# A four-layer graph network on one core: two products moved to ScalarE, a row load moved back, weight rows spread through DRAM, two steps of layer 3 moved

## The chip, the cores and the metric

The kernel runs on one core of a Trainium2 chip. The metric is the device time of one execution in microseconds. Three runs of the kernel before gave 1193.82, 1193.92 and 1194.11 us; the median, 1193.92 us, is the time that the prediction starts from. TensorE (PE) multiplies matrices, VectorE (DVE) and ScalarE (ACT) work on tiles element by element, SyncE (SP) issues nearly all transfers, and 16 DMA engines carry them.

## What is computed

Four graph layers with a residual each, over N = 4096 nodes with D = 128 features and a 4096 x 4096 float32 adjacency of which about one entry in a thousand is not zero.

```python
h = relu(layernorm(x)); x = x + L0(h, adj)   # weighted mean over neighbours, then W and relu
h = relu(layernorm(x)); x = x + L1(h, adj)   # 2 attention heads, layernorm, ff, elu
h = relu(layernorm(x)); x = x + L2(h, adj)   # 1 attention head
h = relu(layernorm(x)); x = x + L3(h, adj)   # adj.T @ h, divided by the column sums
# attention: e = leaky_relu(src[:, None] + dst[None, :]); e = where(adj > 0, e, -9e15)
#            out = softmax(e, axis=1) @ h
```

## The kernel before, in words

**Tiling.** The adjacency is cut into T = 32 tiles of 128 rows along the contracted side and Q = 4 quarters of 1024 columns. A pass of the kernel runs over one quarter and, inside it, over k = 0 to 31. There are five such layers of passes, numbered by `h`: 0 is the reference's L0, 1 and 2 are the two heads of its L1, 3 is its L2, 4 its L3. In this text "layer 0" to "layer 4" are these. In layers 0 and 3 the adjacency tile is the stationary operand, and a tile takes 8 products with 129 columns of G (`products`, L539). In layers 1, 2 and 4 G is stationary, and a tile takes two products with 512 columns (`wide_products`, L555). A float32 product is two instructions, so a tile is 16 instructions of the narrow kind or 4 of the wide.

**Layer 0.** SP loads the tile of k (512 KB) into one of eight slots of the mask area; for the last quarter, where that area fills up, the slots are given by hand (`HOMES`): parts of `ring`, of `U` and of idle parts of `G`. PE multiplies with it, and DVE turns it into an 8-bit mask that is kept on the chip (`masks`, L1405) and from which layers 1 to 3 build their attention tiles. SP loads the tile of k only when PE has used and DVE has masked the tile of k - 8: both engines hold the loads back.

**Attention.** DVE makes a tile E of exponentials with one instruction, max(row, rank) times mask (`run` of DVE, L1367), into one of 4 or 5 slots; PE consumes it and gives the slot back. `row` is a row of scores broadcast over the partitions, and G is scaled in each partition by an exponential v (`scale_g`). At the first quarter of layers 1 and 3 the scores of the last quarter of nodes are not known yet. So tiles 0 to 23 (`EARLY` = 24) go by an early maximum, and before tile 24 the late steps make the right maximum (`top_of`), scale the last part of G (`scale_g(h, 3)`), and correct the running sums (`scale_sums`, L1305 and L1316). The raw row for this is loaded twice, for the early part and as `late_home` for the late one (`load_raw`, L422).

**Hooks.** Each engine's program is one list. `at(ks, steps)` hangs the steps of other work (the last quarter's normalisation, statistics, projections) behind tile k of the running pass, in the order given; the lists `ks` are written by hand. Post-work of a quarter runs over DVE, ACT and PE by turns: for instance the statistics of `post1` (DVE), a root (ACT), `scal` (DVE, L1185), a normalisation (ACT, L829), a transpose on PE (`turned`, L570).

**The weights' rows.** At the second quarter of layer 0, PE's hook 3 projects the weights, and DVE's hook 4 (`place_back`) puts four columns of 128 values into `qcol`. PE's hook 6 (`spread_dots`, L703 and L566) transposes each column, broadcast, into PSUM, so that every partition has it as a row, and DVE's hook 9 (`keep_dots`, L1429) copies the rows to the chip's memory. DVE's dot products of layer 1's feed (`dots`, L1216, from hook 17 on) read them.

Of the kernel before, what the change touches and what calls it, by code (L numbers as in the profile page):

```python
# [30 lines left out]
P = 128  # L31
ALU = mybir.AluOpType
ACT = mybir.ActivationFunctionType
F32 = mybir.dt.float32
# [30 lines left out]
def graph_layers(nc, x, adj, adj_t, diag, alpha, w0_t, bias0, ff0, ff0_t, ff1_t, attn, g1, b1, g2, b2,  # L65
                 w2, w2_t, a2, out, inputs1):
    N, D = x.shape
    T = N // P
    Q = 4
    S = T // Q  # L70
# [19 lines left out]
    with ExitStack() as ctx:  # L90
# [3 lines left out]
        def sem(name):  # L94
            return ctx.enter_context(nc.semaphore(name))
# [8 lines left out]
        ident = sb("ident", [P, P])  # L104
        given_blocks = nc.dram_tensor("given_blocks", (P, T * P), U8, kind="Internal").ap()
        given_rows = nc.dram_tensor("given_rows", (3, N), F32, kind="Internal").ap()
        raw_rows = nc.dram_tensor("raw_rows", (2, QC), F32, kind="Internal").ap()
        ff1T = sb("ff1T", [P, HEADS, D])
        score1 = sb("score1", [P, T, 4])
# [98 lines left out]
        f_var, f_dev, f_scale, f_norm = sem("f_var"), sem("f_dev"), sem("f_scale"), sem("f_norm")  # L208
        f2_var, f2_dev, f2_scale, f2_in = sem("f2_var"), sem("f2_dev"), sem("f2_scale"), sem("f2_in")
        h_turned, h_wide, h_projected, h_placed = sem("h_turned"), sem("h_wide"), sem("h_projected"), sem("h_placed")  # L210
        dots_spread, dots_kept = sem("dots_spread"), sem("dots_kept")
        f_turned, f_wide, f_projected, f_placed = sem("f_turned"), sem("f_wide"), sem("f_projected"), sem("f_placed")

        top_placed, top_spread, bias_made, row_shifted = sem("top_placed"), sem("top_spread"), sem("bias_made"), sem("row_shifted")
# [133 lines left out]
        def _(sp):  # L348
# [15 lines left out]
            def layer0(q, some=range(T)):  # L364

                L = FIRST
                for k in some:
                    if q > 0 and k == 12:
                        keep_own(q - 1)
                    if last_of(q):  # L370
                        home, before = HOMES[k], last_in(HOMES[k], k)
                        if before is not None:
                            sp.wait_ge(*read0(q, before))
                            sp.wait_ge(mask_made, q * T + before + 1)
                        elif home >= MASK:
                            sp.wait_ge(*read0(q - 1, T - FIRST + home - MASK))
                            sp.wait_ge(mask_made, q * T - FIRST + home - MASK + 1)
                        elif home == SUMS:
                            sp.wait_ge(post_done, q)
                    elif k >= L:  # L380
                        sp.wait_ge(slot_used, q * (T - 1) + k - L + 1)
                        sp.wait_ge(mask_made, q * T + k - L + 1)
                    elif 0 < q:
                        if k == L - 1:
                            sp.wait_ge(acc_summed[NB - 1], q)
                        else:
                            sp.wait_ge(slot_used, q * (T - 1) + k - L + 2)
                        sp.wait_ge(mask_made, q * T + k - L + 1)
                    sp.dma_start(tile0(q, k), span(adj_t[k * P:(k + 1) * P, :], q * QC, QC)).then_inc(loaded0(q, k)[0], 16)
# [31 lines left out]
                sp.wait_ge(raw_written, 16 * fixes[h])  # L421
                sp.dma_start(home, raw_rows[fixes[h] - 1].partition_broadcast(P)).then_inc(raw_loaded, 16)  # L422

            layer0(1)
            layer0(2, range(FIRST))
            write_raw(1)
            layer0(2, range(FIRST, T))
            layer0(3, range(2 * S + 2))
            sp.wait_ge(slot_used, (Q - 1) * (T - 1) + S)
            load_raw(1, rows_home[1, 0])  # L430
            layer0(3, range(2 * S + 2, 3 * S + 2))
            sp.wait_ge(slot_used, (Q - 1) * (T - 1) + 2 * S)
            load_raw(1, late_home[1])
            layer0(3, range(3 * S + 2, T))


            sp.wait_ge(f_placed, 2 * Q - 1)
# [92 lines left out]
        def _(pe):  # L530
# [33 lines left out]
            def spread(col, dst):  # L564

                return pe.transpose(dst, col.broadcast_to([P, P]), ident[:, :])  # L566
# [63 lines left out]
            def run(h, q, hooks):  # L630
                n = q + h * Q
                for k in range(T):
                    if h == 0:
                        pe.wait_ge(*loaded0(q, k))
                        if fixed(q) and q == 0 and k < S:
                            if k < HALF - 1:
                                pe.wait_ge(h_placed, k + 1)
                            elif k <= HALF:
                                pe.wait_ge(f_norm if k < HALF else f_placed, 1)
                        elif fixed(q) and q == 0 and k % S == 0:  # L640
                            pe.wait_ge(f_placed, k // S + 1)
                        lhs, used = tile0(q, k), slot_used
                    elif h == 4:
                        pe.wait_ge(*deep(q, k))
                        if fixed(q) and q == 0 and k % S == 0:
                            pe.wait_ge(f_norm, 4 * Q + k // S + 1)
                        lhs, used = stream3[:, k % DEEP, :], deep_used
                    else:
                        pe.wait_ge(e_made, (n - Q) * T + k + 1)
                        if fixed(q) and q == 0 and k % S == 0:  # L650
                            if h == 2:
                                pe.wait_ge(f_norm, 2 * Q + k // S + 1)
                            else:
                                pe.wait_ge(g_scaled[k // S], fixes[h])
                        lhs, used = edges(h, q)[k % len(edges(h, q))], e_used
                        if k == 0 and h != 2 and not (fixed(q) and q == 0):
                            pe.wait_ge(fixed_v, fixes[h])
                    fix = fixes[h] if h in fixes and fixed(q) and q == 0 else 0
                    before = None if fixed(n) and n == 0 else taken(h, q - 1) if not (fixed(q) and q == 0) else taken(h - 1, Q - 1)
                    if h in (1, 2, 4):  # L660
                        wide_products(before, k, lhs, G[:, h % 2, k, 0:P], used, fix)
                    else:
                        products(before, k, lhs, G[:, h % 2, k, :], used, fix, narrow_after=fixed(n) and n == 3 * Q)
                    if k in hooks:
                        hooks[k]()
# [38 lines left out]
                pe.matmul(mix[:, 2, 0:4], affine, qv[:, 0:4], start=True, stop=True, skip_group_check=True)\  # L704
                    .then_inc(back_summed, 1)

            def spread_dots():
                pe.wait_ge(back_placed, 1)
                for c in range(4):
                    mm = spread(qcol[:, c:c + 1], mix[:, 0, c * P:(c + 1) * P])  # L710
                mm.then_inc(dots_spread, 1)
            run(0, 1, {3: turn_weights_back, 6: spread_dots})
            for q in range(2, Q - 1):
                run(0, q, {})
            run(0, Q - 1, {23: lambda: spread_top(early_top[1])})
# [102 lines left out]
        def _(act):  # L818
# [127 lines left out]
            def early_exponentials(h):  # L946

                s_ = SLOPE[h]
                act.wait_ge(bias_made, early_top[h])
                act.activation(G[:, h % 2, 0:EARLY, D], rank[h][:, 0:EARLY], ACT.Exp, bias=vbias, scale=s_).then_inc(v_made, 1)  # L950
                act.activation(rank[h][:, 0:EARLY], rank[h][:, 0:EARLY], ACT.Exp, bias=wbias, scale=1.0 - s_).then_inc(w_made, 1)
                row_exponentials(h, rows_home[h, 0], kept_rows[h] - 1)
# [140 lines left out]
            act.wait_ge(affine_made, 1)  # L1093
            quarters(act, 1, Q - 1, stage0)
            early_exponentials(1)


            post0(Q - 1)
# [53 lines left out]
        def _(dve):  # L1152
# [165 lines left out]
            def scale_g(h, part):  # L1318

                if part == 0:  # L1320
                    dve.wait_ge(v_made, early_top[h])
                elif part == Q - 1:
                    dve.wait_ge(v_made, late_top[h])
                gp = G[:, h % 2, part * S:(part + 1) * S, :]
                v = gp[:, :, D:D + 1].broadcast_to([P, S, D])
                dve.tensor_tensor(gp[:, :, 0:D], gp[:, :, 0:D], v, ALU.mult).then_inc(g_scaled[part], 1)
# [92 lines left out]
            def place_back():  # L1419
# [4 lines left out]
                for c, i in enumerate((1, 3, 0, 2)):  # L1424
                    ins = dve.tensor_copy(qcol[:, c:c + 1], mix[:, 2, i:i + 1])
                ins.then_inc(back_placed, 1)
            def keep_dots():
                dve.wait_ge(dots_spread, 1)
                dve.tensor_copy(w0T, mix[:, 0, 0:P])  # L1429
                dve.tensor_copy(spare[:, o:o + 3 * D], mix[:, 0, P:4 * P]).then_inc(dots_kept, 1)  # L1430
                dve.wait_ge(dots_kept, 1)

            def small_turn(p):

# [40 lines left out]
            def stage0(q, more={}):  # L1475
                post, fed = post0(q - 1), feed(1, q - 1 + Q, q - 1)
                ks = [2,3,5,6,20,7,8,9,10,10,12,14,15,17,18] if last_of(q) else [2, 3, 5, 6, 22, 7, 8, 10, 12, 12, 14, 17, 19, 20, 22]
                masks(q, beside(at(ks, post + fed), more))
            stage0(1, {4: place_back, 9: keep_dots})
            quarters(dve, 2, Q - 2, stage0, st, STAGE0)  # L1480
            early = early_of(1)
            stage0(Q - 1, {21: early[0], 24: early[1], 30: lambda: scale_g(1, 0), 31: lambda: scale_g(1, 1)})


            def post1(h, q):
# [112 lines left out]
                dve.wait_ge(mean_spread, 1)  # L1598
                dve.tensor_copy(mean2, mixed[:, 0:D]).then_inc(mean_kept, 1)
            last = post1(1, Q - 1)  # L1600
            ks = [3,4,5,7,8,14,14,14,16,17,21,22,23,24,25,27]
            run(3, 0, at(ks, last + feed(3, 4 * Q - 1, Q - 1) + late_steps(3) + [mean_of_all, keep_mean]))


# [124 lines left out]
```

## Time and profile before

| what | value |
|---|---|
| median of three runs | 1193.92 us |
| the profiled execution's own time | 1193.39 us |
| its span, first to last instruction | 1191.6 us |
| PE matmuls busy | 1185.7 us, 100% |
| DVE busy | 938.3 us, 79% |
| ACT busy | 325.5 us, 27% |
| granted TensorE clock, mean | 1.000 |
| DMA engines busy, by 40 slices | 8 or 9 tenths in the first eight slices (layer 0) and in the last quarter, 0 to 3 between |

Span and own time differ by 1.8 us, which lie around the first and the last instruction. A busy share says which engine to look at, not what one edit is worth. That is read from the timeline around the edit: which engine waits there, for what, and what comes next.

### The profile page before, as it was taken

Reading aid. Unit: us, or ns where it says so; the run is one execution under the profiler, and the core shown is the slowest. Engines: PE = TensorE matmul, PEld = TensorE weight load, DVE = VectorE, ACT = ScalarE, POOL = GpSimd, SP = SyncE. Lnnn points to the kernel's source line nnn. Section 1 sums busy time; section 2 is a strip of 40 time slices with the busy share of each in tenths; the row PEclk is TensorE's granted clock in tenths of the full one; section 3 lists DMA queues with packets and bytes.
Section 4 is the critical chain, followed back from the end, with each engine's and each line's share of the span. In section 5 each row is a group of like instructions: output and inputs, shape, how many; then the busy total and the mean of one; then the engine's idle time right before and its main releaser. Section 6 shows DMA issues by size and latency. Waiting matters only on the chain.

```text
span 1191.6 us, 16721 instructions
## 1 busy us (share of the span) xinstructions
PE 1185.7 (100%) x6235; PEld 816.7 (69%) x6235; DVE 938.3 (79%) x1677; ACT 325.5 (27%) x780; POOL 9.6 (1%) x20
## 2 busy tenths in 40 slices
PE   9999999999999999999999999999999999999999
PEld 9999999954444444444454547999999964444455
DVE  5548585798979787889797787788787869887786
ACT  4512122225323242423445234541212121000000
POOL 3000000000000000000000000000000000000000
DMA  9888898800111102110010101032303068999920
GB/s 324 304 279 291 248 347 305 282 29 15 40 18 37 18 35 35 53 18 22 1 22 0 40 1 40 1 108 90 141 0 141 1 268 304 313 329 322 322 82 18
DMA packets 90227, 156.30 MB, mean 131 GB/s; under 512 B 45904, under 2 KB 54448, under 8 KB 90160
## 3 DMA queue, kind: packets, MB, share of 16 engines
q1 hardware_dynamic: 64240, 148.58, 36.3%
q10 hardware_dynamic: 25456, 6.30, 2.4%
q8 instruction: 42, 0.69, 0.2%
q0 software_dynamic: 464, 0.53, 0.2%
q14 instruction: 25, 0.20, 0.1%
HBM read 146.94 MB, written 4.78 MB: 127 GB/s over the span
## 4 chain that ended last, share of the span: by engine, by line
PE 94%; DVE 4%; ACT 1%; DMA 0%; issue 0%; DVEq 0%; ACTq 0%
PE acc L555 48%; PE acc L539 36%; PE acc L802 4%; DVE ring L1367 2%; PE mix L621 1%; PE mix L593 1%; PE mix L608 1%; PE acc L810 1%; PE turn L570 1%; DMA ring<-in_adj_t 0%; DVE G L1367 0%; PE mix L670 0%; ACT V L829 0%; DVE stats L1170 0%; ACT U L829 0%
## 5 line engine op out<-in xcount | busy, mean ns | idle before, releaser
L1367 DVE SCALAR_TENSOR_TENSOR ring<-G,score,mask 128x1024 f32<-128x1024 f32 x372 | 466.8, 1280 | 70.9 <-PE acc L555 38.7
L555 PE MATMUL acc<-ring,G 128*128 128x512 f32 x1000 | 436.3, 593 | 0.3 <-DVE acc L1305 0.2
L555 PEld LDWEIGHTS acc<-ring,G 128*128 128x128 f32 x1000 | 186.5, 190 | 229.6 <-issue 210.9
L539 PE MATMUL acc<-G,ring 128*128 128x129 f32 x2240 | 253.9, 275 | 0.8 <-DVE acc L1316 0.7
L539 PEld LDWEIGHTS acc<-G,ring 128*128 128x128 f32 x2240 | 251.9, 192 | 2.1 <-DVE ring L1367 2.0
L539 PE MATMUL acc<-G,mask 128*128 128x129 f32 x1648 | 185.8, 275 | 0.0
L539 PEld LDWEIGHTS acc<-G,mask 128*128 128x128 f32 x1648 | 184.8, 192 | 0.0
L555 PE MATMUL acc<-mask,G 128*128 128x512 f32 x384 | 165.8, 593 | 0.0
L1637 DVE TENSOR_TENSOR ring<-ring,mask 128x1024 f32<-128x1024 f32 x120 | 146.8, 1223 | 11.0 <-DVE ring L1637 0.5
L555 PEld LDWEIGHTS acc<-mask,G 128*128 128x128 f32 x384 | 72.6, 190 | 91.0 <-issue 89.8
L1405 DVE TENSOR_SCALAR mask<-mask 128x1024 uint8<-128x1024 f32 x103 | 68.4, 689 | 27.4 <-DMA mask<-in_adj_t 26.8
L841 ACT ACTIVATE dev<-var 128x8 f32<-128x8 f32 x28 | 5.9, 210 | 217.0 <-DVE var L1179 217.0
L1023 ACT COPY U<-acc 128x512 f32<-128x512 f32 x22 | 12.9, 586 | 172.1 <-PE acc L555 172.1
L802 PE MATMUL acc<-mask,G 128*128 128x384 f32 (+1 forms) x128 | 48.6, 540 | 0.0
L1031 ACT COPY U<-acc 128x387 f32<-128x387 f32 (+1 forms) x24 | 10.4, 446 | 131.6 <-PE acc L539 130.8
L802 PEld LDWEIGHTS acc<-mask,G 128*128 128x128 f32 x128 | 24.2, 190 | 24.0 <-issue 15.6
L829 ACT ACTIVATE V<-X,shift,scale 128x128 f32<-128x128 f32 (+1 forms) x88 | 35.1, 480 | 0.0
L825 ACT ACT_TABLE_LOAD x26 | 33.4, 1283 | 2.7 <-ACT V L829 1.6
L821 ACT COPY cols<-ident 128x1 f32<-128x1 f32 x40 | 7.6, 190 | 86.0 <-DVE V L1216 23.4
L829 ACT ACTIVATE V<-U,shift,scale 128x128 f32<-128x128 f32 x64 | 25.5, 481 | 5.2 <-DVE shift L1189 5.2
L1216 DVE SCALAR_TENSOR_TENSOR V<-G,ring 128x128 f32<-128x128 f32 x96 | 21.4, 290 | 5.3 <-ACT G L829 5.2
L1405 DVE TENSOR_SCALAR mask<-ring 128x1024 uint8<-128x1024 f32 x18 | 12.1, 690 | 10.7 <-PE acc L539 8.7
(207 smaller groups left out, 707.0 us busy)
## 6 DMA issues: line engine op xcount, KB each, us to landing
mask<-in_adj SPq DMA_DIRECT2D x128, 512.0 KB, 5.5
mask<-in_adj_t SPq DMA_DIRECT2D x103, 512.0 KB, 5.2
ring<-in_adj_t SPq DMA_DIRECT2D x18, 512.0 KB, 6.4
G<-given_rows SPq DMA_DIRECT2D x10, 512.0 KB, 3.9
G<-in_adj_t SPq DMA_DIRECT2D x4, 512.0 KB, 6.4
G<-raw_rows SPq DMA_DIRECT2D x4, 512.0 KB, 5.2
inputs<-V ACTq DMA_DIRECT2D x4, 512.0 KB, 2.7
V<-inputs SPq DMA_DIRECT2D x4, 512.0 KB, 3.9
```

The lines of the kernel that those rows point to most:

```text
L539: mm = pe.matmul(acc[:, b, (s % 3) * DW:(s % 3) * DW + DW], lhs[:, s * P:(s + 1) * P], g, start=(k == 0 and s % 3 == 0), stop=(k == T - 1) ...
L555: mm = pe.matmul(acc[:, c, :], g, moving[:, c * BANK:(c + 1) * BANK], start=(k == 0), stop=(k == T - 1), skip_group_check=True)
L570: mm = pe.transpose(turn[:, s * P:(s + 1) * P], V[:, s, :], ident[:, :])
L593: mm = pe.matmul(dst, U[:, s * P:(s + 1) * P], weights, start=True, stop=True, skip_group_check=True)
L802: mm = pe.matmul(acc[:, c, 0:n], G[:, 0, k, 0:P], stream3[:, k, c * BANK:c * BANK + n], start=(k == 0), stop=(k == T - 1), skip_group_chec ...
L825: act.activation(warm[func], ident[:, 0:1], func)
L829: ins = act.activation(dst(s), src(s), func, bias=add(s), scale=mul(s))
L1023: act.copy(U2[:, c, :], acc2[:, c, :]).then_inc(acc_taken, 1)
L1216: ins = dve.scalar_tensor_tensor(V[:, s, :], blocks(G[:, 1, :, :], q, 1, s)[:, 0, 0:D], 1.0, dot_w[c], ALU.mult, ALU.mult, accum_out=block ...
L1367: dve.scalar_tensor_tensor(slots[k % L], late_home[h] if early and k >= EARLY else rows_home[h, q], rank[h][:, k:k + 1], span(mask, (q * T ...
L1405: dve.tensor_scalar(span(mask, (q * T + k) * QC, QC), tile0(q, k), 0.0, None, ALU.is_gt).then_inc(mask_made, 1)
L1637: dve.tensor_tensor(added, stream3[:, 0, :] if k == 1 else added, stream3[:, k, :], ALU.add).then_inc(tile_added, 1)
```

## The change

Four edits, quoted below with the lines that matter.

1. **G of layer 1.** The products of its parts 0 and 1 with v are taken from the end of DVE's list in the last quarter of layer 0 (hooks 30 and 31, one instruction each over 1024 columns) and given to ACT behind the early exponentials, in 8 instructions of 128 columns each for a part.
2. **The late raw row.** SP issued its load between tiles 25 and 26 of the last quarter of layer 0; it now issues it behind tile 31.
3. **The weights' rows.** PE's four transposes and DVE's two copies go. SP writes `qcol` to DRAM as four rows, behind tile 15 of the second quarter, issues tiles 16 and 17, waits until the write has landed, and loads the rows back, broadcast to all partitions, in two transfers. DVE waits for them at the hook at which it had copied, 9.
4. **Layer 3, first quarter.** On DVE the step `scal` moves from hook 8 to 7, and the late step with the maximum (`top_of`) and `scale_g(3, 3)` come at hook 23 together (before: 22 and 23).

```diff
+        dot_rows = nc.dram_tensor("dot_rows", (4 * P,), F32, kind="Internal").ap()
@@ SP
-            layer0(1)
+            layer0(1, range(T // 2))
+            sp.wait_ge(back_placed, 1)
+            sp.dma_start(dot_rows.rearrange("(c p) -> p c", p=P), qcol, allow_slow_non_contiguous=True).then_inc(dots_written, 16)
+            layer0(1, range(T // 2, T // 2 + 2))
+            sp.wait_ge(dots_written, 16)
+            sp.dma_start(w0T, dot_rows[0:P].partition_broadcast(P)).then_inc(dots_loaded, 16)
+            sp.dma_start(spare[:, o:o + 3 * D], dot_rows[P:4 * P].partition_broadcast(P)).then_inc(dots_loaded, 16)
+            layer0(1, range(T // 2 + 2, T))
@@ SP
-            layer0(3, range(2 * S + 2, 3 * S + 2))
+            layer0(3, range(2 * S + 2, T))
             sp.wait_ge(slot_used, (Q - 1) * (T - 1) + 2 * S)
             load_raw(1, late_home[1])
-            layer0(3, range(3 * S + 2, T))
@@ PE
-            def spread_dots():
-                pe.wait_ge(back_placed, 1)
-                for c in range(4):
-                    mm = spread(qcol[:, c:c + 1], mix[:, 0, c * P:(c + 1) * P])
-                mm.then_inc(dots_spread, 1)
-            run(0, 1, {3: turn_weights_back, 6: spread_dots})
+            run(0, 1, {3: turn_weights_back})
@@ ACT
             early_exponentials(1)
+            scale_g(1, 0)
+            scale_g(1, 1)
@@ DVE
-            def keep_dots():
-                dve.wait_ge(dots_spread, 1)
-                dve.tensor_copy(w0T, mix[:, 0, 0:P])
-                dve.tensor_copy(spare[:, o:o + 3 * D], mix[:, 0, P:4 * P]).then_inc(dots_kept, 1)
-                dve.wait_ge(dots_kept, 1)
+            def dots_there():
+                dve.wait_ge(dots_loaded, 32)
@@ DVE
-            stage0(1, {4: place_back, 9: keep_dots})
+            stage0(1, {4: place_back, 9: dots_there})
-            stage0(Q - 1, {21: early[0], 24: early[1], 30: lambda: scale_g(1, 0), 31: lambda: scale_g(1, 1)})
+            stage0(Q - 1, {21: early[0], 24: early[1]})
@@ DVE, run(3, 0)
-            ks = [3,4,5,7,8,14,14,14,16,17,21,22,23,24,25,27]
+            ks = [3, 4, 5, 7, 7, 14, 14, 14, 16, 17, 21, 23, 23, 24, 25, 27]
```

## Rows read from the trace of the kernel before

**Rows 1.** The page, part 1: busy time, share of span, instructions.
```profile
PE 1185.7 (100%) x6235; PEld 816.7 (69%) x6235; DVE 938.3 (79%) x1677; ACT 325.5 (27%) x780; POOL 9.6 (1%) x20
```

**Rows 2.** Timeline of PE: start us, us, engine, line, tiles, [idle before <-releaser].
```profile
246.87 3.60 PE L555 MATMUL acc<-ring,G 128*128 128x512 f32 x8
250.31 1.88 PE L555 MATMUL acc<-G 128*128 128x512 f32 x4
...
268.46 1.98 PE L555 MATMUL acc<-G 128*128 128x512 f32 x4 [0.82 <-DVE G L1367]
...
279.54 1.09 PE L582 MATMUL turn<-ident,G 128*128 128x128 f32 x8
...
746.72 1.09 PE L570 MATMUL turn<-ident,V 128*128 128x128 f32 x8 [0.43 <-ACT V L829]
...
777.59 2.05 PE L539 MATMUL acc<-G,ring 128*128 128x129 f32 x16
...
780.49 3.95 PE L539 MATMUL acc<-G,ring 128*128 128x129 f32 x32 [0.74 <-DVE acc L1316]
```

**Rows 3.** Timeline of PE around the four transposes of the weights' rows.
```profile
87.31 0.60 PE L566 MATMUL mix<-ident,ring 128*128 128x128 f32 x4
87.75 52.42 PE L539 MATMUL acc<-G,mask 128*128 128x129 f32 x468
```

**Rows 4.** Timeline of DVE, second quarter of layer 0: hook 9, masks 10 and 13.
```profile
90.84 0.28 DVE L1429 COPY ring<-mix 128x128 f32<-128x128 f32 x1
...
91.63 0.69 DVE L1405 TENSOR_SCALAR mask<-mask 128x1024 uint8<-128x1024 f32 x1
...
98.77 1.29 DVE L1405 TENSOR_SCALAR mask<-mask 128x1024 uint8<-128x1024 f32 x2
```

**Rows 5.** Views of lines L417 and L389: raw row's write, then the tile of 136.2.
```profile
L417 SPq DMA_DIRECT2D raw_rows<-score x1: 426/426/426, 133.0 to 133.0; - x1
DMA to landing us min/median/max: 9.8/9.8/9.8
...
DMA to landing us min/median/max: 10.7/10.7/10.7
```

**Rows 6.** The same view: the 28 tiles issued from 80 to 130 us.
```profile
DMA to landing us min/median/max: 4.4/4.8/5.8
```

**Rows 7.** The same view: the tile issued at 224.0, into an empty queue.
```profile
DMA to landing us min/median/max: 3.8/3.8/3.8
```

**Rows 8.** Timeline of DVE, end of layer 0, start of layer 1.
```profile
240.51 0.69 DVE L1405 TENSOR_SCALAR mask<-ring 128x1024 uint8<-128x1024 f32 x1 [0.59 <-DMA ring<-in_adj_t]
...
242.85 1.22 DVE L1326 TENSOR_TENSOR G<-G 128x1024 f32<-128x1024 f32 x1
243.99 2.48 DVE L1367 SCALAR_TENSOR_TENSOR ring<-G,score,mask 128x1024 f32<-128x1024 f32 x2
...
247.58 2.48 DVE L1367 SCALAR_TENSOR_TENSOR ring<-G,score,mask 128x1024 f32<-128x1024 f32 x2
```

**Rows 9.** Timeline of ACT in the same stretch.
```profile
246.03 1.41 ACT L1031 COPY U<-acc 128x387 f32<-128x387 f32 x3 [9.83 <-PE acc L539]
...
256.45 2.43 ACT L983 ACTIVATE G<-G 128x128 f32<-128x128 f32 x8
```

**Rows 10.** Timeline of DVE, first quarter of layer 3, around hooks 7 and 8.
```profile
741.85 1.28 DVE L1367 SCALAR_TENSOR_TENSOR ring<-G,score,mask 128x1024 f32<-128x1024 f32 x1
743.04 0.20 DVE L1185 RECIPROCAL scale<-dev 128x8 f32<-128x8 f32 x1
```

**Rows 11.** Timeline of DVE and ACT, the same quarter, around hooks 22 to 24.
```profile
773.40 0.16 DVE L1269 TENSOR_REDUCE cols<-score 128x1 f32<-128x8 f32 x1 [2.17 <-ACT score L939]
...
776.26 1.28 DVE L1367 SCALAR_TENSOR_TENSOR ring<-G,score,mask 128x1024 f32<-128x1024 f32 x1
...
779.78 1.36 DVE L1316 TENSOR_TENSOR acc<-acc,ring 128x387 f32<-128x387 f32 x3
...
776.38 1.06 ACT L944 ACTIVATE G<-G 128x1024 f32<-128x1024 f32 x1
```

More of the change, by code:

```diff
@@ L210, in graph_layers @@
         h_turned, h_wide, h_projected, h_placed = sem("h_turned"), sem("h_wide"), sem("h_projected"), sem("h_placed")
-        dots_spread, dots_kept = sem("dots_spread"), sem("dots_kept")
+        dots_written, dots_loaded = sem("dots_written"), sem("dots_loaded")
         f_turned, f_wide, f_projected, f_placed = sem("f_turned"), sem("f_wide"), sem("f_projected"), sem("f_placed")
```

## The prediction

> **What bounds the kernel.** I read the page first, then the timeline of PE for gaps, and last the timelines of DVE, ACT and SP around each gap. PE is busy for 1185.7 us [rows 1] of the 1191.6 us span, and its clock is at full level. So an edit pays only if it takes instructions off PE or closes one of its gaps. The gaps are few. In layer 1, the 8 wide matmuls of two tiles take 250.31 - 246.87 = 3.44 us [rows 2], 1.72 a tile. Tile 12 is due at 246.87 + 12 x 1.72 = 267.5 and starts at 268.46 [rows 2], 0.96 late. The turn behind tile 17 is due at 246.87 + 18 x 1.72 = 277.8 and starts at 279.54 [rows 2], 1.7 late. In layer 3, PE waits 0.43 for ACT before the turn at 746.72, then for tile 23 (777.59, some 0.25 late), then 0.74 for the corrected sums (780.49) [rows 2]. With the time until the next first matmul, the layer 3 gaps come to 0.59, 0.25 and 0.90. Elsewhere PE is fed: 468 narrow matmuls in 52.42 us are 0.112 us each [rows 3], which 16 to a tile makes 1.79 us.
>
> **Part A, PE's four transposes.** They start at 87.31 and the next matmul at 87.75 [rows 3]: 0.44 us of PE, with nothing beside it. Gain 0.44, certain.
>
> **Part B, what takes their place.** This is SP, DRAM and a wait on DVE, and the cost has to be worked out as a chain; times are on the clock of before, PE 0.44 early. PE's tile 7 starts at 87.3 and ends at 89.1; SP issues tile 15 then and the element write at about 89.8. The trace has one such write in the same setting, the raw row's: 1024 values of 4 bytes at 133.0, landed 9.8 us later; the tile issued 3.2 us behind it took 10.7 [rows 5] against 4.8 in the calm stretch [rows 6], so 5.9 more. Ours has 512 values. If the hold-up goes by the count, it is half: landed 5.9 us after issue or so (2 us to get through the queue, half of the other 7.8), at 95.7; tile 17, issued at 92.9, lands at 92.9 + 4.8 + 2.9 = 100.6. The two loads are issued at 96, stand behind it in the queue, and 256 KB are half a tile. **The rows are there at about 101**, between 98 (write soon through) and 107 (below).
>
> Before, mask 10 came at 91.63 [rows 4]. So DVE stands at hook 9 for some 9 us. Behind it are the masks, and behind those SP's loads, since tile k needs mask k - 8. From mask 10 to mask 13 are 98.77 - 91.63 = 7.14 us, with ACT's normalisation between, and 0.6 for mask 13 itself [rows 4]: tile 21 can be issued 8.0 us after the rows are there. By then the queue is empty, and a tile takes 3.8 [rows 7], so it lands 11.9 us after them with the signal. PE wants tile 21 at 87.31 + 14 x 1.79 = 112.3. **The point from which this wait counts is therefore rows at 100.4**; at 101 it costs 0.6 us. Tiles 18 to 20 have 2 us or more of slack; from tile 22 on the loads follow at 1.3 us or less against PE's 1.79, so the stall is paid once. DVE's two copies (from 90.84 to 91.63 [rows 4]) are saved where DVE waits anyway: nothing. Cost of B: 0.6, from 0 to 6.4.
>
> **Part C, start of layer 1.** The first tile E starts at 243.99, when both products (the second at 242.85, 1.14 us) are done [rows 8]. Without them E0 comes behind mask 31. That needs tile 31's landing. Tile 30 landed at 240.5 [rows 8]; mask 31 ran right behind the first product at 242.25, so tile 31 was there by then, and without the raw row ahead of it not later. With mask 31 at 242.25 still, E0 would start at 242.85, 1.14 early. With landing at 241.0, E0 to E3 are made by 246.5, and E4 waits for its slot until PE has read its tile 31 (some 0.2 behind 246.87 [rows 2], so 247.1), where before it ended at 247.58 + 2.4 = 249.97 [rows 8]: 248.3, 1.67 early. DVE is busy without a gap from there to PE's stalls, so **the chain comes 1.1 to 1.7 early, I take 1.5**, since moving the 512 KB row away frees about 1.3 us of the queue ahead of the last tiles. PE can use up to 1.7 (above). What is late next is the turn behind tile 17, by 0.2. Gain C: 1.5.
>
> The cover of the moved work: ACT makes 8 instructions for a part in 2.43 us [rows 9], so both take 4.9 us. It stood idle for 9.83 us before 246.03 [rows 9], behind one copy of 1.15 us; both fit, and PE needs part 0 at 246.87 only. Without that cover, all 4.9 us would stand ahead of the copy of the sums that PE waits for at the start of layer 1. On the rows ACT needs 2.43 us for what DVE does in 1.14. The Trainium skill ("ScalarE: Activation LUTs", Rules for kernel authors) says that multiplications belong on VectorE, which is faster per element. By that rule the edit would lose 2.6 us if ACT were bound here; the trace agrees with the rule on the price, and the idle time makes it free.
>
> The late raw row is now issued near 237 and first used by the late step, which comes behind the turn of 279.54 [rows 2]; it is late for nobody. SP's commands behind it (the weight of layer 3, the last own blocks) shift by less than a microsecond.
>
> **Part D, layer 3.** `scal` at hook 7: DVE now waits about 0.5 us for ACT's root instead of making E8 first (741.85), and the scale comes at about 742.35 in place of 743.04 [rows 10]. ACT's normalisation and PE's turn follow 0.7 earlier, and the gap of 0.59 closes. E8 ends near 743.9; PE wants it at 746.72 - 0.59 - 1.79 = 744.3. The late step at hook 23: DVE stood idle for 2.17 us before 773.40 [rows 11], and E23 now fits there, so PE does not wait for it (0.25). Behind the maximum, at 776.26 [rows 11], come the product (1.14) and E24, which needs ACT's row at 777.44 [rows 11]: 777.5 to 778.7. The sums are corrected from 778.7, not from 779.78 [rows 11], and PE, which ends tile 23 at 777.34 + 1.79 and turns the rows in 0.11, starts tile 24 at 779.25 rather than 780.49. Then E25 is made only at 781.2 and PE is there at 781.0: 0.2 comes back, against 0.2 that PE lost there before. Gain D: 0.59 + 1.24 = 1.8; bounds 1.0 (E8 or E25 late by 0.8 together) and 2.0.
>
> **Sum** against the profiled execution's own 1193.39: -0.44 + 0.6 - 1.5 - 1.8 = -3.1, which gives 1190.3. The median lies 0.53 above the profiled one, so **1190.8 us**. A difference that can be told from none is 0.2%, 2.4 us.
>
> **Rivals.**
>
> 1. *The element write does not go by its count.* If the 4-byte writes queue for the same stretches of memory, 512 hold up the engines as long as 1024 did. Then the write lands at 99.6 and tile 17 at 92.9 + 10.7 = 103.6 [rows 5], the rows are there at about 104.4, and PE stalls for 4.0 at tile 21. Sum: -0.44 + 4.0 - 3.3 = +0.3, so 1194.2, no difference. For it: the trace has no write of another count; against it: nothing but the plausibility of a cost per value. The Trainium skill ("DMA: Bandwidth & Descriptors", Queues, rings and completion order) says that a transfer's signal lands only after all earlier writes of the same DMA engine. The trace agrees as far as it goes: the tile behind the raw write landed late too [rows 5].
> 2. *Slower: DVE's wait at hook 9.* If in addition the loads, issued only when the write has landed (99.6), take the 7 us that a transfer has in a disturbed queue (the mean of 3.8 [rows 7] and 10.7 [rows 5]), the rows are there at 106.8. DVE's wait holds mask 13, mask 13 holds tile 21, and PE stalls for 106.8 - 100.4 = 6.4. Sum: -0.44 + 6.4 - 3.3 = +2.7, 1196.6. It ends slower than before from rows at 104.1, slower by 0.2% from 106.5. Against it: small reads behind a write that has landed stand in a calm queue.
> 3. *The wait is hidden.* If the write lands in 4 us, the rows come by 100 and B costs nothing; with C at 1.67: -0.44 - 1.7 - 1.9 = -4.0, 1189.9.
> 4. *C or D does not do what it says*: another link of the chain (ACT's root, the slot of an E tile) holds PE at the same place. With half of 3.3 lost, 1192.4, no difference.
>
> **How the numbers follow.** Forecast (B between 0 and 1.3) 0.42, rival 3 0.15, rival 1 (stall of 1.3 to 5) 0.22, rival 4 0.12, rival 2 0.09. The forecast's own spread is 1190.2 to 1191.5, just under the threshold of 1191.5. Faster by over 0.2%: 0.42 and 0.15, 0.57. Within: rivals 1 and 4, 0.34. Slower: rival 2, 0.09. The range goes from 1189.8 (rival 3) to 1194.4 (rival 1), and leaves out rival 2 and the upper tail of rival 1.
>
> **What would show it.** In the changed trace: no transposes at 87 and PE's tiles 0.44 early; DVE idle before mask 10 with a DMA as releaser, for about 9 us; a PE gap at tile 21 of the second quarter, waiting for a DMA, of about 0.6; the first E tile 1.1 to 1.7 earlier against PE's first wide matmul, and no PE gap at tile 12; no gap at the turn of layer 3, and tile 24 some 1.2 us earlier against tile 22. The prediction is wrong if the rows arrive after 102, if ACT's products delay its copy of layer 0's last sums, or if E8 or E25 now hold PE.

## The result and the profile after

| kernel | median, us | against before |
|---|---|---|
| before, in the runs beside it | 1194.01 | 1 |
| the whole change | 1197.24 | 1.0031 (95% interval 1.0023 to 1.0039) |

**Slower by 3.2 us, where 3.1 us faster was forecast.** The profiled execution of the changed kernel took 1198.24 us with a span of 1196.4. The kernel before was measured again beside each group of runs, and its median moved by up to 1.1 us between them (1192.88 to 1194.01); so each kernel is compared with the runs of the kernel before made beside it.

PE's timeline of the second and third quarter of layer 0, after the change (start us, us, engine, line, tiles, [idle before <-releaser]):

```profile
83.27 25.26 PE L546 MATMUL acc<-G,mask 128*128 128x129 f32 x224
111.07 2.05 PE L546 MATMUL acc<-G,mask 128*128 128x129 f32 x16 [2.54 <-DMA mask<-in_adj_t]
113.59 3.84 PE L546 MATMUL acc<-G,mask 128*128 128x129 f32 x32 [0.47 <-DMA mask<-in_adj_t]
118.58 7.56 PE L546 MATMUL acc<-G,mask 128*128 128x129 f32 x64 [1.16 <-DMA mask<-in_adj_t]
126.32 13.89 PE L546 MATMUL acc<-G,mask 128*128 128x129 f32 x122 [0.17 <-DMA mask<-in_adj_t]
...
152.41 17.77 PE L546 MATMUL acc<-G,mask 128*128 128x129 f32 x154 [0.81 <-DMA mask<-in_adj_t]
```

From tile 4 at 83.27 the four transposes are gone [rows 3], and 14 tiles run through. Then PE waits for tiles 18, 19, 21 and 25. Tile 25 is due at 83.27 + 21 x 1.787 = 120.8 and starts at 126.32: **5.5 us lost in the second quarter**. Tile 7 of the third is due 14 tiles later, at 151.3, and starts at 152.41: 1.1 more, and 0.3 follow at the tiles behind it. Before, nothing was lost in either [rows 3]. A check on the whole is PE's next instruction that is no product with a tile. It comes 84 tiles after tile 4, in the last quarter; here in the changed kernel, and before together with tile 4:

```profile
240.36 0.27 PE L573 MATMUL mix<-ident,cols 128*128 128x128 f32 x1
```
```profile
81.87 5.61 PE L539 MATMUL acc<-G,mask 128*128 128x129 f32 x48
...
232.47 0.27 PE L566 MATMUL mix<-ident,cols 128*128 128x128 f32 x1
```

It comes 240.36 - 83.27 = 157.09 us behind tile 4, before 232.47 - 81.87 = 150.60 with the 0.44 of the transposes in it. **So 6.9 us are lost in layer 0, some 5.5 in the second quarter and 1.4 in the third.**

DVE's timeline at hook 9, and the view of the transfers of the rows:

```profile
91.64 0.69 DVE L1409 TENSOR_SCALAR mask<-mask 128x1024 uint8<-128x1024 f32 x1
106.48 0.69 DVE L1409 TENSOR_SCALAR mask<-mask 128x1024 uint8<-128x1024 f32 x1 [14.15 <-DMA ring<-dot_rows]
```
```profile
L427 SPq DMA_DIRECT2D dot_rows<-ring x1: 427/427/427, 91.1 to 91.1; - x1
L430 SPq DMA_DIRECT2D ring<-dot_rows x1: 327/327/327, 101.0 to 101.0; - x1
L431 SPq DMA_DIRECT2D ring<-dot_rows x1: 426/426/426, 101.3 to 101.3; - x1
...
DMA to landing us min/median/max: 4.0/5.1/9.9
```

The write (L427) took the 9.9 us; the loads were issued when it had landed and took 4.0 and 5.1 us, and DVE stood for 14.15 us where before it copied for 0.8 and went on [rows 4].

The start of layer 1 and the first quarter of layer 3, PE and one row of DVE:

```profile
250.54 2.48 DVE L1371 SCALAR_TENSOR_TENSOR ring<-G,score,mask 128x1024 f32<-128x1024 f32 x2 [0.21 <-DVE mask L1409]
```
```profile
254.77 3.60 PE L562 MATMUL acc<-ring,G 128*128 128x512 f32 x8
...
286.13 1.09 PE L589 MATMUL turn<-ident,G 128*128 128x128 f32 x8
...
750.93 1.95 PE L546 MATMUL acc<-G,ring 128*128 128x129 f32 x16
752.72 1.04 PE L577 MATMUL turn<-ident,V 128*128 128x128 f32 x8
...
785.33 3.95 PE L546 MATMUL acc<-G,ring 128*128 128x129 f32 x32
```

The first E tile stands 254.77 - 250.54 = 4.23 us ahead of PE's first wide matmul, before 246.87 - 243.99 = 2.88 [rows 2, 8]. From that matmul to the turn behind tile 17 are 31.36 us, before 279.54 - 246.87 = 32.67 [rows 2]: **1.3 gained**. In layer 3 the turn follows its tile by 1.79, which is no gap (0.59 before), and from the turn to tile 24 are 32.61 us, before 33.77 [rows 2]: **1.75 gained**. So the sum of the profiled executions is -0.44 + 6.9 - 1.3 - 1.75 = +3.4. The rest of their difference of 4.85 lies ahead of the change: tile 4 of the second quarter starts at 83.27, before at 81.87, 1.4 earlier. That start lay between 81.3 and 83.8 in the profiles of this study, whichever edits a kernel had.

### The profile page after: what moved, and what is told of

The parts are those of the page before. It is cut to its first block, busy times and chain, and to the rows that moved or that the text cites. A ratio compares the mean times of both kernels' runs of the same rounds, so it can differ in the third digit from the quotient of the medians.

```text
span 1196.4 us, 16728 instructions
## 1 busy us (share of the span) xinstructions
PE 1186.1 (99%) x6231; PEld 816.1 (68%) x6231; DVE 935.0 (78%) x1673; ACT 331.0 (28%) x796; POOL 9.6 (1%) x20
## 4 chain that ended last, share of the span: by engine, by line
PE 90%; DMA 5%; DVE 3%; ACT 1%; issue 0%; DVEq 0%; ACTq 0%
PE acc L562 48%; PE acc L546 33%; DMA mask<-in_adj_t 4%; PE acc L804 4%; PE mix L628 1%; DVE ring L1371 1%; PE mix L615 1%; PE mix L600 1%; PE acc L812 1%; ACT U L866 0%; DMA ring<-in_adj_t 0%; PE turn L577 0%; DVE G L1371 0%; ACT G L831 0%; PE mix L677 0%; ACT V L831 0%
## 5 line engine op out<-in xcount | busy, mean ns | idle before, releaser
L1058 ACT ACTIVATE U<-V,cols 128x512 f32<-128x512 f32 x8 | 6.1, 808 | 51.6 <-DMA V<-U 51.6
```

## The experiments

Each kernel below has one profiled execution, and sizes of gaps are from that one; the times are medians where nothing else is said. Code is cut to the lines that matter.

Theory: the way through DRAM is the loss, by DVE's wait, the masks and SP's loads; the three other edits do what they say. Rivals: another edit costs as well, or the slow write holds the tiles up whatever DVE does.

### Edits 1, 2 and 4 without the way through DRAM

Against the changed kernel (PE's function and SP's lines of edit 3 are put back as well):

```diff
-            run(0, 1, {3: turn_weights_back})
+            run(0, 1, {3: turn_weights_back, 6: spread_dots})
...
-            stage0(1, {4: place_back, 9: dots_there})
+            stage0(1, {4: place_back, 9: keep_dots})
```

> Edits 1, 2 and 4 alone: the weights' rows are spread by PE and copied by DVE as before. Theory (the slowdown is the way through DRAM: DVE's wait for the rows at hook 9 holds the masks and by them SP's tile loads, and PE stalls 5 to 6 us in layer 0; the other edits do what they say): 1191.0 us, 3.0 below before, with no PE gap over 0.5 us in the second quarter of layer 0, none at tile 12 of layer 1 and none before the turn of layer 3. Rival (one of the other edits costs time as well): 1193 us or more.

Measured 1190.65 us against 1193.24, ratio 0.9978 (0.9969 to 0.9987). PE's waits, all of them:

```profile
PE mix L669 <- DVE V L1376: 1.1, 1, 1.1
PE mix L592 <- ACT U L863: 0.7, 1, 0.7
PE acc L538 <- DMA mask<-in_adj_t: 0.3, 1, 0.3
PE acc L554 <- DVE acc L1306: 0.2, 1, 0.2
```

The waits of layers 1 and 3 of before [rows 2] are gone; the one for a tile's DMA is in the first quarter, at 27.6 us, and the second has none. The other edits are a gain of 2.6 us; the rival about them falls.

### Edit 3 alone

> Edit 3 alone. Theory: PE stalls at tiles 18 to 31 of the second quarter, 5 to 6 us in sum, less 0.44 for the transposes: 1199.0 us, 5 above before, and the gaps of layers 1 and 3 as before. Rival (the stalls are shared between this edit and the others): under 1197 us.

Measured 1199.44 us against 1193.24, ratio 1.0049 (1.0035 to 1.0062): 6.2 us, where 5 were expected. Its profile shows less than the expected 5 to 6 us in the second quarter, 3.8, and 1.4 that were not expected in the third; that is 4.8 with the transposes taken off, so over a microsecond of the 6.2 is not found in these gaps (the interval runs from 4.2 to 7.4). The two runs add up: 6.2 - 2.6 = 3.6, and the whole change measured 3.2.

### DVE waits at hook 16 instead of 9

Against the changed kernel, the whole edit:

```diff
-            stage0(1, {4: place_back, 9: dots_there})
+            stage0(1, {4: place_back, 16: dots_there})
```

> The whole change, but DVE waits for the rows at hook 16, right ahead of the first dot products, instead of hook 9. The write and the loads stay where they are. Theory (it is DVE's wait that holds the masks and so the loads, not the write itself): PE's stalls in the second quarter go, under 0.5 us is left, and the time is 1190.5 us, 3.5 below before. Rival (the 4-byte writes hold up the DMA engines, and the tiles come late whatever DVE does): PE still stalls 3 us or more, and the time is 1194 us or more.

Measured 1190.20 us against 1193.24, ratio 0.9976 (0.9967 to 0.9986). All of PE's waits, and DVE's mask behind the wait:

```profile
PE mix L677 <- DVE V L1379: 1.1, 1, 1.1
PE acc L562 <- DVE acc L1309: 0.2, 1, 0.2
```
```profile
105.86 0.69 DVE L1409 TENSOR_SCALAR mask<-mask 128x1024 uint8<-128x1024 f32 x1 [3.92 <-DMA ring<-dot_rows]
```

The write was as slow as before (10.0 us to land), and DVE again was held until 105.9, but now behind 17 masks instead of 10. SP could load on, and PE never stood. **The slow write costs nothing where nothing but the dot products waits for it.** This kernel beats both the kernel before and the changed one; it cannot be told from the one without DRAM (1190.65, beside the same runs of before).

### DVE's wait without any write

Against the kernel with edits 1, 2 and 4 alone:

```diff
-            stage0(1, {4: place_back, 9: keep_dots})
+            stage0(1, {4: place_back, 9: lambda: (keep_dots(), dve.wait_ge(slot_used, T - 1 + 17))})
```

> Edits 1, 2 and 4 with PE's transposes and DVE's copies as before, no way through DRAM at all, but behind its copies at hook 9 DVE waits until PE has read tile 16 of the second quarter, which is 7.1 us before tile 21 is due, as late as the rows came in the whole change. Theory (DVE's wait by itself, by way of the masks and the loads, is the stall): PE stalls 4.5 to 5.5 us in the second quarter, and the time is 1195.5 us, 5 above the same kernel without the wait. Rival (the slow write or the loads behind it take part): under 3 us of stall. For the second stall, in the third quarter: if it comes from DVE being late, the raw row's write there takes 14 us and PE stalls 1 us or more; if it comes from the small write a quarter earlier, 9 to 11 us and no stall.

Measured 1198.23 us against 1192.88, ratio 1.0045 (1.0029 to 1.0062), 7.9 us above the same edits without the wait (each against its own runs of before: +5.35 and -2.6). DVE at hook 9, then PE:

```profile
105.29 0.69 DVE L1406 TENSOR_SCALAR mask<-mask 128x1024 uint8<-128x1024 f32 x1 [14.29 <-issue]
```
```profile
87.17 19.82 PE L538 MATMUL acc<-G,mask 128*128 128x129 f32 x176
...
110.33 10.65 PE L538 MATMUL acc<-G,mask 128*128 128x129 f32 x80 [3.35 <-DMA mask<-in_adj_t]
121.44 30.64 PE L538 MATMUL acc<-G,mask 128*128 128x129 f32 x272 [0.46 <-DMA mask<-in_adj_t]
```

With PE's transposes and no write, a hold of 14.3 us on DVE gives the same stall, at tile 18 first: 5.8 us in the second quarter, 5.6 in the changed kernel. The wait by itself is enough for that loss. The third quarter's loss came too (1.3 us of gaps), with a raw row's write of 13.6 us. The time is over the expectation by 2.7 us, of which the gaps explain about 2.

### The write two tiles earlier

Against the changed kernel:

```diff
-            layer0(1, range(T // 2))
+            layer0(1, range(T // 2 - 2))
...
```

with the write behind it as in the change, and the loads behind tile 16, so that three tiles instead of two are issued between write and loads.

> The whole change with DVE's wait at hook 9, but SP issues the write of the four columns behind tile 13 instead of 15 (3.6 us earlier) and the loads behind tile 16. Theory (a threshold: PE stalls by as much as the rows come later than 11.9 us before tile 21 is due): the rows come 3.6 us earlier against PE's tiles, DVE's wait at hook 9 falls from 14.2 to some 10.6 us, PE's stalls in the second quarter fall from 5.0 to 1.4 us, and the time to 1193.5 us. Rival (the 4-byte write as such holds up the tiles): the stall stays at 3 us or more and the time over 1195 us.

Measured 1193.55 us against 1193.32, ratio 1.0002 (0.9993 to 1.0011). DVE's mask behind the wait:

```profile
101.67 0.69 DVE L1409 TENSOR_SCALAR mask<-mask 128x1024 uint8<-128x1024 f32 x1 [10.37 <-DMA ring<-dot_rows]
```

The stall of the second quarter fell to 1.6 us, near the 1.4 expected. The third quarter's was 1.9, about what it was in the changed kernel.

The threshold of the prediction can be checked on all of them. PE's gaps are summed from the spacings of its matmuls over 0.15 us, less the usual 0.112. "Rule" is the mask's start at hook 9 plus 11.85, less the time at which tile 21 is due.

| kernel | mask 10 starts | tile 21 due | rule | gaps, 2nd quarter | gaps, 3rd quarter |
|---|---|---|---|---|---|
| whole change | 106.48 | 113.65 | 4.7 | 5.6 | 1.4 |
| edit 3 alone | 104.66 | 113.24 | 3.3 | 3.8 | 1.4 |
| 128 values | 105.02 | 113.42 | 3.5 | 4.7 | 1.0 |
| raw rows placed first (below) | 105.94 | 112.6 | 5.2 | 6.0 | 2.5 |
| wait without write | 105.29 | 112.2 | 4.9 | 5.8 | 1.3 |
| write earlier | 101.67 | 112.62 | 0.9 | 1.6 | 1.9 |
| 16 bytes apart | 101.22 | 113.55 | below 0 | 0.4 | 3.3 |
| 64 bytes apart | 99.34 | 113.28 | below 0 | 0.1 | 0.0 |
| 512 bytes apart | 98.11 | 112.03 | below 0 | 0.1 | 0.8 |

Where it gives a stall, the rule is right to within 1.2 us and always low. It took the first late tile to be 21, while at a wait of 12.7 us or more tile 18 is late already: in the changed kernel that tile landed 4.6 us after the mask's start at hook 9, but it is due 5.4 us ahead of tile 21. And the two tiles issued next took 5.1 and 5.8 us to land, not 3.8.

### What makes the write slow

Four kernels change the write. In all, the loads bring three or four rows into which SP wrote the vector `bias0` at the start, instead of the weights' rows, so their outputs are not the reference's; the diffs show the write alone.

```diff
-            sp.dma_start(dot_rows.rearrange("(c p) -> p c", p=P), qcol, ...)
+            sp.dma_start(dot_rows[0:P].rearrange("(c p) -> p c", p=P), qcol[:, 0:1], ...)
```

> The whole change, but SP writes one of the four columns (128 values of 4 bytes instead of 512; the other three rows are filled from a weight at the start, so the dot products of three rows are not the reference's). 512 values took 9.9 us from issue to landing, 1024 values 9.8. Theory 1 (the time goes by the count of values behind a fixed 2 us): 4 us or less. Theory 2 (values that lie side by side are written one behind another, 16 to a stretch of 64 bytes, and that sets the time): 9 to 10 us again, and DVE waits as long as before. Theory 3 (the write waits for the tiles ahead of it and is not slow itself): 5 to 6 us.

```diff
+            sp.dma_start(apart_rows.rearrange("(c p w) -> p c w", p=P, w=16)[:, :, 0], qcol, ...)
```

> The whole change, but the 512 values are written 64 bytes apart into an area of their own (the rows that are loaded back were filled from a weight at the start, so the dot products are not the reference's). Theory 2 (values side by side in one stretch are written one behind another; 128 values took 8.7 us, 512 took 8.5 to 10.0, 1024 took 9.8): with one value to a stretch of 64 bytes the write lands in 3 to 4 us. Rival (a fixed price of every 4-byte write to DRAM behind tiles in the queue, whatever the layout): 8 us or more.

The same with `w=128`:

> As values_64_bytes_apart, with the values 512 bytes apart (the dot products again are not the reference's). Theory 2: 3 to 4 us, as with 64 bytes; if the stretch within which writes wait for one another is longer than 64 bytes, this run is fast and the other is not. Rival (a fixed price): 8 us or more in both.

The same with `w=4`:

> As values_64_bytes_apart, with the values 16 bytes apart, four to a stretch of 64 bytes (the dot products again are not the reference's). Side by side, 16 to 64 bytes, the write took 8.5 to 10.0 us; 64 and 512 bytes apart 4.9 and 4.7. Theory (writes to one stretch follow one another at a fixed price each): (9.5 - 4.9) / 15 = 0.3 us a value, so 4.9 + 3 x 0.3 = 5.8 us, and no PE stall. Rival (any sharing of a stretch costs all of it): 8.5 us or more, and PE stalls 3 us or more.

The rows of the write and the time to landing, in the order: 128 values side by side (the last of the three numbers is the write's), then 512 values 64, 512 and 16 bytes apart:

```profile
L430 SPq DMA_DIRECT2D dot_rows<-ring x1: 383/383/383, 90.9 to 90.9; - x1
...
DMA to landing us min/median/max: 3.3/4.6/8.7
```
```profile
L431 SPq DMA_DIRECT2D apart_rows<-ring x1: 385/385/385, 90.7 to 90.7; - x1
...
DMA to landing us min/median/max: 4.9/4.9/4.9
```
```profile
L431 SPq DMA_DIRECT2D apart_rows<-ring x1: 386/386/386, 89.5 to 89.5; - x1
...
DMA to landing us min/median/max: 4.7/4.7/4.7
```
```profile
L431 SPq DMA_DIRECT2D apart_rows<-ring x1: 386/386/386, 91.0 to 91.0; - x1
...
DMA to landing us min/median/max: 6.2/6.2/6.2
```

| values | apart | to 64 bytes | landed after |
|---|---|---|---|
| 1024 (raw row, before) | 4 bytes | 16 | 9.8 us [rows 5] |
| 1024 (second raw row, before, at 600.6 us, no tiles in the queue) | 4 bytes | 16 | 11.1 us |
| 512 (five executions) | 4 bytes | 16 | 8.5 to 10.7 us |
| 128 | 4 bytes | 16 | 8.7 us |
| 512 | 16 bytes | 4 | 6.2 us |
| 512 | 64 bytes | 1 | 4.9 us |
| 512 | 512 bytes | 1 | 4.7 us |

**The count does not matter; how many values share a short stretch of memory does.** 128 values took 8.7 us, as 512 did in two of five executions, and 512 values at 64 bytes took half of the 9.9. Rows with values apart are from one execution each, and executions of one and the same write differ by up to 2.2 us, so 4.9 against 8.5 or more stands clear, 6.2 against 4.9 less so. The price of 0.3 us for each further value in a stretch of 64 bytes, taken from the first and the last case, gave 5.8 us for the case between, and 6.2 was measured; a stretch of 32 bytes would give 5.6, so its length is not shown. Whether the write is slow itself, or only what is queued ahead of it, the DMA engines' traffic shows: first the changed kernel, then values 64 bytes apart (stretch of time, its length, the engines' busy time, clock, DMA share, GB/s):

```profile
91.10:94.00 2.90, 2.90 (x29) 2.90 (x28) 1.16 (x6) 0.21 (x1) 0.00 (x0) 1.00 0.88 293
94.00:96.00 2.00, 2.00 (x21) 2.00 (x20) 0.00 (x0) 0.00 (x0) 0.00 (x0) 1.00 1.27 265
96.00:101.00 5.00, 5.00 (x48) 5.00 (x47) 0.00 (x0) 0.00 (x0) 0.00 (x0) 1.00 0.86 42
```
```profile
95.60:97.00 1.40, 1.40 (x15) 1.40 (x14) 0.00 (x0) 0.00 (x0) 0.00 (x0) 1.00 0.89 334
```

The 4-byte packets begin some 2.5 us after the issue in both kernels and are over about 5 us after it. Side by side, the engines then moved 42 GB/s for 5 us until the write landed; with 64 bytes between them they went on at 334. So about 2.5 us are the queue, and the hold-up stands behind the packets. That writes to one stretch follow one another is what this looks like; the trace does not show it being done. The Trainium skill ("DMA: Bandwidth & Descriptors", Why small descriptors are slow) states a fixed overhead for each packet and each descriptor. By that overhead alone 512 values would cost the same at any distance, and 128 a quarter. The runs show neither.

Of the expectations, the 9 to 10 us for 128 values (8.7) and the 3 to 4 us for values far apart (4.9 and 4.7) were missed by 0.3 to 0.9 us.

In single executions the kernel with 128 values took 1196.90 us against 1193.24, and the two kernels with values far apart took 1190.72 and 1190.21 us against 1193.32, with DVE's wait still at hook 9 (7.4 us long). The one with 16 bytes took 1194.48 against 1193.67: its second quarter was nearly free of gaps (0.4), but its third had 3.3 us of them, so "no PE stall" was a miss.

### The third quarter

> The whole change with the two small DRAM areas declared in the other order, so that the raw rows lie where they lay before the change. If the place in memory makes the raw row's write slow (14.4 us against 9.8), it falls to 9 to 11 us and PE's stall of the third quarter goes; if not, it stays at 14 us. The stall of the second quarter stays at 4 to 6 us in either case.

Measured 1198.71 us in one execution, with gaps of 6.0 and 2.5 us in the second and third quarter, and the raw row's write at 13.7 us. The place in memory is not it. The write took 9.3 to 11.7 us in the kernels whose DVE is not held at hook 9 (before, edits 1, 2 and 4 together and alone, wait at hook 16), 12.2 and 12.7 with the values far apart, and 13.6 to 15.5 in the rest (the profile of the one with 128 values lacks it), the one without any small write ahead of it among them. So it goes with DVE being held a quarter earlier. The traces show part of the way. These are the DMA packets in the 5 us after the raw row's write was issued (before, the changed kernel, the wait without a write):

```profile
DMA packets 1389, 1.27 MB, mean 255 GB/s; under 512 B 1079, under 2 KB 1079, under 8 KB 1389
```
```profile
DMA packets 548, 1.98 MB, mean 397 GB/s; under 512 B 64, under 2 KB 64, under 8 KB 548
```
```profile
DMA packets 560, 2.03 MB, mean 406 GB/s; under 512 B 64, under 2 KB 64, under 8 KB 560
```

The write's own small packets come from 2.7 us on before, and only from 5.7 us on in the changed kernel: the queue ahead of the write is fuller, since SP is still loading tiles close behind one another to catch up (14 in the 18.1 us ahead of it, against 8 in 12.8 before). That is 3 of the 4.6 us by which the write lands later. Why the rest is longer, and that the tiles behind the write are late by it and not otherwise, no run tests.

### The other edits one by one

> Edit 1 alone, the raw row's load where it was. Theory (the first E tile of layer 1 comes earlier by what the products took on DVE, less the wait for the last tile): E tiles 1.1 to 1.5 us earlier against PE, PE's gap of 0.8 at tile 12 gone, 1192.3 us, 1.2 below before. Rival (without the load moved the last tile lands too late for any gain): the gap stays over 0.5 us.

Measured 1192.38 us against 1193.32, ratio 0.9992 (0.9983 to 1.0001): 0.9 us less, which the times alone do not tell from none. In the trace, PE from the first wide matmul to the turn takes 31.58 us, before 32.67 [rows 2]:

```profile
246.91 3.60 PE L555 MATMUL acc<-ring,G 128*128 128x512 f32 x8
...
278.49 1.09 PE L582 MATMUL turn<-ident,G 128*128 128x128 f32 x8
```

The gap of 0.8 at tile 12 is gone.

> Edit 2 alone: the late raw row's load behind tile 31, the products still on DVE. Theory (the load moved away helps only where DVE waits for the last tiles; with the products at hooks 30 and 31 the waits are partly covered): the first E tile at most 0.5 us earlier against PE, PE's gap of 0.8 at tile 12 of layer 1 shrinks to 0.3 to 0.8, and the time is within 0.5 us of before. Rival (the load moved is most of the gain at the start of layer 1): the gap goes, 1192.3 us or less.

Measured 1193.35 us against 1193.67, ratio 0.9999 (0.9989 to 1.0009). The gap at tile 12 is halved and stays:

```profile
268.33 1.98 PE L554 MATMUL acc<-G 128*128 128x512 f32 x4 [0.37 <-DVE G L1366]
```

From the first wide matmul (247.20) to the turn (279.42) are 32.22 us, 0.45 less than before.

> Edit 4 alone. Theory (both steps come earlier than PE's waits): no PE wait before the turn of layer 3, none for the corrected sums, the gap of layer 1 as before, 1.6 to 1.8 us less of PE gaps, 1191.7 us. Rival (E8 or E25 now hold PE): new waits of PE for an E tile, less than 1 us gained.

Measured 1191.96 us against 1193.67, ratio 0.9987 (0.9977 to 0.9997). PE before the turn and at tile 24:

```profile
746.78 1.04 PE L570 MATMUL turn<-ident,V 128*128 128x128 f32 x8
...
779.40 3.94 PE L539 MATMUL acc<-G,ring 128*128 128x129 f32 x32
```

That is 1.7 us less, as expected. Both waits are gone; the two starts are 32.62 us apart, before 33.77 [rows 2]. Together, edits 1 and 2 gave 1.4 us at the start of layer 1 in the kernel without DRAM and 1.7 in the one with the wait at hook 16. Over all ten profiles with both edits it is 0.8 to 1.7, and the two kernels with neither (edit 3 alone, edit 4 alone) lie 0.4 and 0.3 on the other side of before; so this stretch scatters by some 0.4 us from profile to profile.

## Why the prediction was wrong

- **What bounds the kernel**: right. All that was won and lost shows as gaps of PE, or as its transposes.
- **Part A**, 0.44 us: right. The transposes are gone and nothing else stands there.
- **Part B is the step that failed**: 0.6 us were put down and 6.9 were lost. First in it is one term: "If the hold-up goes by the count, it is half". The write was taken at 5.9 us and took 9.9; 128 values took 8.7. Of the 5.9, the 2 us for the queue stood in no row; the packets began after 2.5. On the clock of the prediction (the changed profile runs 1.35 us behind it at this place), the rows came at 105.1, not at 101. Tile 17, put down at 7.7 us to land, took 11.0, as the tile behind the raw row had (10.7 [rows 5]). The way of the loss was described rightly: DVE's wait, mask 13, the loads, PE, with a threshold of 11.9 us ahead of tile 21. At 105.1 that threshold gives 4.7 us, and 5.5 to 5.6 were lost. The prediction had the raw row's 9.8 us before it and divided it by a rule that no row showed. The undivided number would have given rival 1's 4.0 us, and rival 1 said so, but had 0.22.
- **The threshold is low by 0.9 us** here. "Tiles 18 to 20 have 2 us or more of slack" holds for rows at 100.4; on the measured 4.6 us from the mask to the tile's landing, tile 18 is late from rows at about 102.4 on, and it was the first that PE waited for. The stall was not "paid once".
- **A second loss was missing**: 1.4 us in the third quarter. Runs show that it comes with the hold of DVE; the fuller queue ahead of the raw row's write is part of the way, the rest is open.
- **Rival 2**, the slower one, was nearest, with 1196.6 us against 1197.24, but for half a wrong reason. The loads took 5.1 us, not 7.2; the rows came 1.7 us earlier than it said, and the rest came from the other stall and from a threshold that is low by 1 us.
- **Part C**: 1.5 forecast, 1.3 measured in the changed kernel. E0 came 1.35 earlier. ACT took both products without delaying its copy. That the load had to move for the full gain is not shown: 1.1 without, 0.8 to 1.7 with it. The load moved by itself took 0.45 off. And the price of 2.43 us against 1.14 does not show that ACT is slower for each element: it is eight instructions against one, and one instruction of ACT over 128 x 1024 took 1.06 us [rows 11].
- **Part D**: 1.8 forecast, 1.75 measured, the 0.59 before the turn as worked out and 1.16 of the 1.24 up to tile 24. (The 0.90 in its list of gaps is 1.0 by its own rows.)
- **The sum** with B at what it cost: -0.44 + 6.9 - 1.3 - 1.75 = +3.4 in the profiled executions, and the medians moved by 3.2.
- **The range** ended at 1194.4. Rival 1, with the raw row's measured times undivided, gives 1194.2, so the count rule is not all of the miss: the 3 us from there to 1197.24 are, about, the threshold (0.9), the third quarter (1.4), rows 0.7 later than rival 1 had them, and smaller gains of C and D (0.25). The chain had one unknown duration, and its two readings lay on both sides of a threshold; that calls for a range that takes in both readings with all that follows them.

## What to carry to other kernels

A wait that is put on an engine working through its list in order holds all that the engine does next, and by it the loads that wait for that work: put it directly ahead of the first reader. Here seven hooks made the difference between 3.2 us lost and 3.0 us won, with the same slow transfer. And when the trace has one instance of a kind of transfer, take its duration as it stands for another size, until a run has shown that it scales.

## What the runs showed of the hardware that was not expected

- 4-byte writes to DRAM cost by neighbourhood, not by number: 8.5 to 10.7 us for 128 to 1024 values side by side, 6.2 at 16 bytes apart, 4.9 at 64, 4.7 at 512. Some 2.5 us of these times are the queue ahead of the write; without tiles in the queue, 1024 values side by side took 11.1 all the same.
- While such a write is held up the DMA engines move little else: 42 GB/s for 5 us, against 293 ahead of it.
- The tiles behind such a write land late too: 8.9 and 11.0 us for the two issued 1.4 and 3.2 us after it, against 4.8 in a calm stretch [rows 6]. The Trainium skill ("DMA: Bandwidth & Descriptors", Queues, rings and completion order) lets a signal land only after all earlier writes of the same DMA engine; the trace agrees.
- The start of the kernel scatters: tile 4 of the second quarter began between 81.3 and 83.8 us in profiles of kernels that are alike up to there.
